# A three-stage decoder layer on one core: the bulk loads of cross-attention move from SyncE's queue to ScalarE's

## The reference

```
x = layernorm(x + attn(x))          # exp sums of causal scores with rotary positions, then a small two-layer net
x = layernorm(x + xattn(x, ctx, ctx, bias, w_out))
x = layernorm(x + ffn(x))           # 512 -> 2048 -> 512, quantised weights and activations, gelu

xattn: q, k, v = heads(x), heads(ctx), heads(ctx)           # no projections of q, k, v
       logits  = q @ k.T + bias                             # bias: 16 x 2048 x 154, the same for all sequences
       attn    = softmax(logits / sqrt(32)) @ v
       return combine(attn) @ w_out
```

## Time and profile before

| | |
|---|---|
| median of three executions | 2286.98 us |
| the profiled execution | 2296.95 us |
| its span, first to last instruction | 2295.1 us |
| TensorE busy | 2126.5 us, 93% |
| VectorE busy | 1738.3 us, 76% |
| ScalarE busy | 1086.7 us, 47% |
| GpSimd busy | 828.9 us, 36% |
| mean granted TensorE clock | 0.947 of full speed |
| DMA queue of SyncE and of stores and loads by GpSimd | 286.07 MB and 160.28 MB |

### The profile page before, as it was taken

One profiled execution on the slowest core, in us unless ns is written; L12 is line 12 of the kernel. 1 busy time (PEld: TensorE's weight loads), 2 busy tenths in 40 slices (PEclk: granted clock), 3 DMA queues, 4 the chain that ended last, 5 costly groups with the idle time before them and its releaser, 6 DMA issues.

```text
span 2295.1 us, 32921 instructions
## 1 busy us (share of the span) xinstructions
PE 2126.5 (93%) x11880; PEld 1184.2 (52%) x11904; DVE 1738.3 (76%) x3296; ACT 1086.7 (47%) x1522; POOL 828.9 (36%) x802
## 2 busy tenths in 40 slices
PE   7999999984898999999999859999999799999997
PEld 3444444431676777776777624444444344444443
DVE  6768686855677798897898665777656488888885
ACT  1444444443355454555555324444444465555551
POOL 2122221222135455555555342322222134444442
PEclk9999999997589899999999779999999899999999
DMA  6344343456669979979996437888888656666662
GB/s 232 107 136 144 103 143 105 114 137 176 179 145 195 251 167 186 264 187 183 254 212 144 152 81 252 289 284 285 272 270 268 250 200 233 226 225 235 228 224 79
DMA packets 386626, 448.46 MB, mean 195 GB/s; under 512 B 279270, under 2 KB 279430, under 8 KB 368032
## 3 DMA queue, kind: packets, MB, share of 16 engines
q1 hardware_dynamic: 322448, 286.07, 46.5%
q0 software_dynamic: 64016, 160.28, 22.9%
HBM read 258.93 MB, written 138.73 MB: 173 GB/s over the span
## 4 chain that ended last, share of the span: by engine, by line
PE 81%; DVE 6%; DMA 5%; issue 5%; ACT 2%; POOL 1%; DVEq 0%; SPq 0%; POOLq 0%; ACTq 0%
PE ps_h L1658 19%; PE ps L1901 19%; PE ps_proj L568 10%; PE ps_o L1230 8%; PE ps_w L1259 6%; PE ps_s L588 5%; DMA qs<-stack 4%; PE ps_o L1226 3%; PE ps_m L1182 3%; PE ps_m L1184 3%; PE ps_l L1208 2%; DVE rope_t L403 1%; PE ps_t L1244 1%; DVE x_hi L386 1%; PE ps_l L1205 1%
## 5 line engine op out<-in xcount | busy, mean ns | idle before, releaser
L1658 PE MATMUL ps_h<-xT,b_rows 128*128 128x512 f16 x2048 | 444.5, 380 | 12.6 <-DMA xT<-x_lo 12.6
L1901 PE MATMUL ps<-w,g_hi 128*128 128x512 f16 x1024 | 389.1, 380 | 21.1 <-DVE g_lo L1837 21.1
L1901 PE MATMUL ps<-w,g_lo 128*128 128x512 f16 x1024 | 389.1, 380 | 0.0
L1658 PEld LDWEIGHTS ps_h<-xT,b_rows 128*128 128x128 f16 x2048 | 200.9, 98 | 256.0 <-issue 16.1
L1230 PEld LDWEIGHTS ps_o<-vm,pT 128*128 128x128 f32 x2048 | 308.9, 208 | 14.1
L1499 ACT ACTIVATE h<-ps_h,b_in_sb,col_scale 128x512 f32<-128x512 f32 x256 | 199.2, 778 | 241.2 <-PE ps_h L1658 241.1
L1060 DVE TENSOR_REDUCE stack<-ps_m 128x2 f16<-128x308 f32 x512 | 244.3, 479 | 73.0 <-PE ps_m L1184 57.9
L1230 PE MATMUL ps_o<-vm,pT 128*128 128x33 f32 x2048 | 292.7, 270 | 0.0
L1017 ACT ACTIVATE pT<-logit 128x512 f32<-128x512 f32 x320 | 199.7, 626 | 126.2 <-DVE logit L1078 124.9
L1572 DVE TENSOR_REDUCE amax_t<-h 128x1 f32<-128x2048 f32 x64 | 146.2, 2284 | 114.2 <-ACT h L1499 113.8
L1750 POOL TENSOR_TENSOR rstd<-vare,minus_half 128x1 f32<-128x1 f32 x64 | 154.4, 2412 | 208.3 <-DVE vare L1855 208.3
(11 more groups left out here) (179 smaller groups left out, 3858.9 us busy)
## 6 DMA issues: line engine op xcount, KB each, us to landing
hidden<-h POOLq DMA_DIRECT2D x64, 1024.0 KB, 6.8
hT<-hidden SPq DMA_DIRECT2D x64, 1024.0 KB, 6.1
xc<-x_cols SPq DMA_DIRECT2D x16, 1024.0 KB, 5.1
xr<-x_rows SPq DMA_DIRECT2D x16, 1024.0 KB, 5.4
x_rows<-x POOLq DMA_DIRECT2D x16, 1024.0 KB, 4.8
x1t<-x_rows SPq DMA_DIRECT2D x64, 256.0 KB, 3.9
bt_main<-bias_main SPq DMA_DIRECT2D x16, 1024.0 KB, 7.1
xres<-x_rows SPq DMA_DIRECT2D x64, 256.0 KB, 3.8
```

What stands on the lines that cost most here:

```text
L1658: mm = pe.matmul(ps_h[f % 4][:], w1[:, c, f * P:(f + 1) * P], xT[:, e, a, :, c, :], start=(a == 0 and c == 0), stop=(a == 1 and c == KC - 1))
L1901: mm = pe.matmul(ps[t][:], g[:, e, f, t * P:(t + 1) * P], w2[:, f, :], start=(f == 0 and a == 0), stop=(f == FC - 1 and a == 1))
```

## The change

ScalarE gets a function `bulk_loads`, called as the last thing of each of its quarters, behind `token_half`. All loads of the bias, of `kb`, `ks` and of the values are issued there, 109 DMAs in all, in the same quarters by number as before, except that the third and fourth group of the first span's bias come in q = -2 and q = -1 instead of (0, 0) and (0, 1). The waits in front of the loads move with them. The very first `kb` and `ks` loads ahead of the pipeline, all transposes, `x1t`, the residual rows and the output weights stay on SyncE.

```diff
             def quarter(s, b, i):                       # SyncE
-                if 4 * n + i == -4:
-                    for j in range(2):
-                        sp.wait_ge(done.x1_out[j], 16 * done.blocks // 2)
-                    sp.wait_ge(done.ks_out, 16 * done.blocks)
-                    sp.wait_ge(done.kb_out, 16 * done.blocks)
-                    load_bias(0, 0)
-                    load_v(0, 0)
-                if 4 * n + i == -3:
-                    load_bias(0, 1)
-                    load_kb(1, 1)
                 turn_heads(*span_at(s, b, i, 6))
                 turn_stack(*span_at(s, b, i, 4))
...
-                if isinstance(s, int) and n == 0 and i < 2:
-                    load_bias(0, 2 + i)
...
-                if i == 0 and not (isinstance(s, int) and n >= UNITS - 2):
-                    sp.wait_ge(mx_done, 32 * (n + 1))
-                    load_kb((b + 2) % BATCH, b % 2)
...
+            def bulk_loads(n, i):                       # ScalarE
+                s, b = n // 4, n % 4
+                if 4 * n + i == -4:
+                    for j in range(2):
+                        act.wait_ge(done.x1_out[j], 16 * done.blocks // 2)
+                    act.wait_ge(done.ks_out, 16 * done.blocks)
+                    act.wait_ge(done.kb_out, 16 * done.blocks)
+                    load_bias(0, 0)
+                    load_v(0, 0)
+                if 4 * n + i == -3:
+                    load_bias(0, 1)
+                    load_kb(1, 1)
+                if 4 * n + i in (-2, -1):
+                    load_bias(0, i)
+                if not 0 <= n < UNITS:
+                    return
+                if i == 0 and n < UNITS - 2:
+                    act.wait_ge(mx_done, 32 * (n + 1))
+                    load_kb((b + 2) % BATCH, b % 2)
+                if i == 1 and not last(n):
+                    if not first(n):
+                        act.wait_ge(pv_done, 8 * n)
+                    load_ks((b + 1) % BATCH, (b + 1) % 2)
+                    load_v((b + 1) % BATCH, (b + 1) % 2)
+                if s < UNITS // BATCH - 1 and b == BATCH - 1 and i >= 1:
+                    act.wait_ge(biased, 5 * (4 * n + i))
+                    load_bias(s + 1, i - 1)
+                if not first(n) and b == 0 and i == 0:
+                    act.wait_ge(biased, 20 * n)
+                    load_bias(s, GROUPS - 1)
...
                 token_half(*at(n, i, 7))
+                bulk_loads(n, i)
```

More of the change, by code:

```diff
@@ L834, in load_residual @@
                     bass.ds(4 * s + t, 1)].rearrange("n p d -> p (n d)")).then_inc(xres_in[t % 2], 16)
[L836 to L840, removed]
             def load_kb(b, e):
@@ L848, in load_ks @@
                 sp.dma_start(ks[3 * HD:STACK, e], rows[3 * HD:STACK]).then_inc(ks_in[e], 16)
-            def load_v(b, e):
-                sp.dma_start(vm[:, e], v_main[b]).then_inc(v_in[e], 16)
-                sp.dma_start(vt[:, e], v_tail[b]).then_inc(v_in[e], 16)
             sp.wait_ge(done.proj_done, done.jobs)
@@ L891, in quarter @@
                     sp.dma_start(x2t[:], w_chunks[:, 2:4]).then_inc(wo_in, 16)
-                if isinstance(s, int) and n >= UNITS:
-                    return
-                if i == 0 and not (isinstance(s, int) and n >= UNITS - 2):
-                    sp.wait_ge(mx_done, 32 * (n + 1))
-                    load_kb((b + 2) % BATCH, b % 2)
[L897 to L901, removed]
-                if not (isinstance(s, int) and s == UNITS // BATCH - 1) and b == BATCH - 1 and i >= 1:
-                    sp.wait_ge(biased, 5 * (4 * n + i))
-                    load_bias(s + 1, i - 1)
-                if not first(n) and b == 0 and i == 0:
-                    sp.wait_ge(biased, 20 * n)
-                    load_bias(s, GROUPS - 1)
             for q in range(-8, TAIL):
@@ L987, in _, with load_bias, load_kb, load_ks @@
         def _(act):
+            def load_bias(s, g):
+                act.dma_start(bt_main[:, g], bias_main[4 * g:4 * g + 4].rearrange("h k (s t) -> k h s t", t=BLK)[
+                    :, :, bass.ds(s, 1), :].rearrange("k h s t -> k h (s t)")).then_inc(bt_in[g], 16)
+                act.dma_start(bt_tail[:, g], bias_tail[g].rearrange("k (s t) -> k s t", t=BLK)[
+                    :, bass.ds(s, 1), :].rearrange("k s t -> k (s t)")).then_inc(bt_in[g], 16)
+            def load_kb(b, e):
+                act.dma_start(kb[:, e], kb_dram[b]).then_inc(kb_in[e], 16)
+            def load_ks(b, e):
+                rows = ks_dram[b].rearrange("r (h k) -> r h k", h=HEADS)
+                act.dma_start(ks[0:3 * HD, e], rows[0:3 * HD]).then_inc(ks_in[e], 16)
+                act.dma_start(ks[3 * HD:STACK, e], rows[3 * HD:STACK]).then_inc(ks_in[e], 16)
+            def load_v(b, e):
+                act.dma_start(vm[:, e], v_main[b]).then_inc(v_in[e], 16)
+                act.dma_start(vt[:, e], v_tail[b]).then_inc(v_in[e], 16)
             def token_half(nu, t):
```

## The result

Four executions of the changed kernel took 2342.70 to 2347.11 us, median **2343.65 us**. Four of the kernel before took 2285.77 to 2302.94 us, median 2292.35 us. The ratio is **1.0227**, 95% interval [1.0193, 1.0261]: slower, as forecast, but 2306 us was forecast and 2340 was the upper end of the range. (The interval lies wholly above 1; whether the loss is more or less than 2% it leaves open.) The profiled execution took 2347.11 us with a span of 2345.3 us, 50.2 us more than before.

What follows compares the result with a forecast made beforehand. TensorE, busy 93% of the span, was taken as the bound. Fill +11 us and steady part +8 us gave 19 us on 2287, so 2306 us; 8-in-10 range 2270 to 2340, the forecast case alone 2295 to 2326.

Steps and rivals of the forecast that it cites:

- The forecast case: Bulk issued after `token_half` falls on the next quarter's transposes, which land late: +19 us, 2306 us, chance 0.5.
- the own queue gives nothing: Bulk on ScalarE's queue does not protect the transposes, which still land about 2.0 us (1.6 to 2.5) after the last bulk load.
- the fill: Pipeline start, q = -4 to -1: no threshold protects, every microsecond of later `stack` landing lengthens the kernel: +11 us.
- the steady part: Quarters after the pipeline start: `stack` landings above 9.0 us after issue stop TensorE: 3.6 us plus about 4 for scatter, +8.
- The rival of fair turns: Transposes in their own queue land in about 8.6 us, stops at the bias change go: 2271 us, chance 0.2.
- ScalarE held at its issues: ScalarE's issues wait while SyncE is occupied by a `stack` transpose, exponentials run late: 2332 us, up to 2380, chance 0.15.
- plus its time to land: In the `stack` landing formula: the last bulk load's time from issue to landing, put at 5.4, 7.0 or 8.0 us.
- The formula: `stack` landing from its issue: last bulk issue's offset behind L997, its landing time, minus 1.4 (transpose's start), plus 2.0 us.
- The twelve (n,1) without bias: Quarters with four bulk issues: next `stack` transpose lands after 8.9 us, just under the 9.0 us threshold; scatter costs perhaps 0.2 us.
- The (3,1) kind: Quarters (3,1), (7,1), (11,1) with six bulk issues: transpose lands after 10.8 us, surplus 1.8 each, net +1.8 us.
- Scatter at the threshold: In 18 steady quarters whose `stack` landings lie near 9.0 us, variation of the landings costs about 4 us.
- The clock: New TensorE stops may lower the granted clock as in 740 to 780 us: up to 10 us more, only in the bounds.

Runs made afterwards that it cites:

- sp_late: Kernel before, with every steady bulk load issued by SyncE one quarter boundary later, just ahead of the next quarter's transposes; fill as before: ratio 1.0161.
- fill_late_sp: Kernel before, with only the pipeline-fill loads issued one quarter boundary later, still by SyncE, right ahead of the transposes: ratio 1.0069.
- kv_act: fill_sp with all bias loads back on SyncE in their old places; ScalarE issues only `kb`, `ks` and the values: ratio 1.0023.
- fill_sp: Changed kernel with the pipeline-fill loads (q = -4 to -1) back on SyncE in their old places; steady bulk stays late on ScalarE: ratio 1.0124.
- act_mid: fill_sp with ScalarE issuing the bulk in the middle of its quarter, between its second and third exponential: ratio 1.0141.
- fill_act: Kernel before, with only the pipeline-fill loads (q = -4 to -1) on ScalarE as in the changed kernel: ratio 1.0083.
- the spread kernel on SyncE: Kernel before, all bulk on SyncE at its old place in the quarter, but loads spread over different quarters: ratios 0.9905 and, run again, 0.9898.

## Why the prediction was wrong in size

**Direction and mechanism held.** The forecast case was that the bulk falls on the next transposes, that the own queue gives nothing, and that the fill loses more than the steady part by quarter. The traces show the late landings, the own queue gained nothing in any run, and the fill holds half of the new idle time (16.1 of 32.6 us). sp_late and fill_late_sp show that a late issue costs as much without the new queue. The rival of fair turns fell: the transposes issued right behind six bulk loads landed in 14.7, 11.8 and 10.3 us, not under 9.0. So did ScalarE held at its issues: they took 0.30 to 0.68 us but for two (0.83 and 1.64 us), `combT` still waits for `ps_t`, and kv_act costs nothing. It happened twice in fill_sp, in (7,2) and (11,2): the sixth issue took 0.75 and 1.05 us, `combT` was 2.3 and 2.6 us late and TensorE idle for 1.2 and 1.6 us.

**The failed term** is "plus its time to land". The formula was offset of the last bulk issue, plus its time to land, minus 1.4, plus 2.0, and I put in the times of before, 5.4, 7.0 and 8.0 us. Those are times of a load that was issued ahead of the transposes of its queue. Handed over with them, the last bias load took 13.9 us instead of 8.0 and `kb` in the fill 10.2 instead of 7.0: the load is drawn out as well as the transpose. (That the DMA engines take turns between them is how I read these landings; no view shows the turns.) The trace of before had a case of it. The forecast used one `b_rows` load, of 8.8 us; all 12 of that line over the whole span show

```profile
DMA to landing us min/median/max: 8.7/13.0/16.5
```

The one of 16.5 us was issued at 697.65, beside the transpose of 697.40 that took 13.41 us. I had read nearly the shortest. The same work took about as long as before: before, the first bulk issue of this place was at 742.66 and the transpose landed at 759.0, 16.3 us; now 766.07 and 783.5, 17.5 us. What was lost is the head start. With the measured times the formula gives the landing, as it must: `token_half` ended at 767.40, the last issue was at +0.7, it landed in 13.9, the transpose stood at +1.4 and landed 1.5 after it: 0.7 + 13.9 - 1.4 + 1.5 = 14.7 us, as the chain shows. The forecast had 2.2 + 8.0 - 1.4 + 2.0 = 10.8: 1.5 too much for the offset, 5.9 too little for the time to land, 0.5 too much behind it. In the fill: `kb` issued at +0.2 behind the end of L976 (570.18), landed in 10.2, transpose at +1.8 and 1.7 after `kb`: 10.3 us, against 8.5 forecast.

Term by term, idle time of TensorE:
- The fill: forecast +11 us. Measured +16.1 us (39.72 against 23.65 us, first rows of the two tables). The four landings grew by 3.7, 6.1, 1.7 and 5.3 us, where 2.8, 4.2, 2.4 and 2.8 stood (the last counted half).
- The steady part: forecast +8 us, measured +16.5. The twelve (n,1) without bias were priced about right or too high: the transposes behind them that no `b_rows` load disturbed landed in 4.3 to 9.8 us, median 7.6, where 8.9 was forecast, and units 5, 9 and 13, which have little else, stood idle 0.6 us at most. The (3,1) kind was too low, 14.7, 11.8 and 10.3 us for 10.8. The loss in the first quarters of units 3, 7 and 11 wasn't in the sum: 9.5, 10.0 and 11.1 us where 8.9, 9.0 and 7.8 were before. Units 3, 7 and 11 hold 11.1 of the 16.5 us by the two tables. In (3,0) `b_rows` now stood 1.7 us ahead of the transpose where it was 0.8 us behind it before; in the other two it isn't so, and no run settles it.
- Scatter at the threshold was 4 us of the sum; nothing in the trace asks for it.

**The clock** was left out of the sum and held for up to 10 us of the bounds. It was 17.3 us in the two profiles, a third of the loss. In the fill the granted clock fell from 0.65 to 0.56, in units 7 and 11 from 0.93 to 0.84 and from 1.00 to 0.93; in unit 3, which has the longest new stop behind the fill, it was 0.87 before and 0.90 after, so not each stop costs clock where it stands. That step, a stop priced as its idle time only, is the second one that failed. The bounds have a slip beside it: their lower end is 2287 + 10 = 2297 us, not 2295.

Sum: 32.6 + 17.3 = 49.9 us measured, 19 forecast. Of the 31 us missing, 5 are the fill, 8 or 9 the steady landings, and 17 the clock.

**What the theory lacked.** That a separate queue gives nothing was too kind. act_mid shows a transpose that was issued ahead of its bulk and took 16.2 us all the same, and at equal amounts of bulk ScalarE is 1.4% behind SyncE. How much of those 1.4% is the queue and how much the later issue isn't separated: the spread was not run on SyncE with late issues.

## What to carry to other kernels

When loads move, ask first at what moment they are handed over and which latency-bound transfer is issued next; price both together as one amount of work from the first issue to the last landing, never with the time that the load took in another place. A queue in order can be a protection: in (3,0), (7,0) and (11,0) SyncE came to its `kb` load only 5.0 to 6.7 us behind the transpose, while a second queue let it start 1.5 us behind. If a bottleneck lies in bursts, spread the bursts (here 1% by moving four loads to other quarters), and price new stops of TensorE with the clock that they cost beside the idle time.

## What the runs showed of the hardware

- **In the trace ScalarE's DMAs leave ahead of its own pending activation.** In the program the issue of line 960 stands behind L976. In the trace it is at 766.07, 0.7 us before L976 starts (766.79) and 1.3 us before it ends. So the bulk came some 1.5 us less late than the forecast assumed.
- **An issue on ScalarE is short**, 0.30 to 0.68 us in 107 of 109. In the changed kernel none of them fell into the time that a `stack` transpose occupies SyncE; in act_mid the `kb` issue of 732.65 did, 3.7 us into 7.30, and took 0.33 us.
- **The clock's low stretch behind the fill varies between executions.** The profiled executions of the kernel before and of the changed one ran unit 1 partly at the lower clock, those of fill_sp, kv_act and fill_act wholly at the upper one. That this isn't the change shows in the spread kernel on SyncE, which was profiled twice. Unit 1 in its first execution and in its second:

```profile
625.82:661.83 36.01, 35.81 (x302) 28.85 (x299) 30.60 (x72) 23.87 (x40) 10.60 (x10) 1.00 0.74 164
...
628.88:674.33 45.45, 45.41 (x317) 36.45 (x316) 32.63 (x74) 23.91 (x40) 10.59 (x10) 0.80 0.60 130
```

The kernel before:

```profile
629.25:674.71 45.46, 45.36 (x317) 36.41 (x316) 32.66 (x74) 24.04 (x40) 10.59 (x10) 0.80 0.62 130
```

  The difference, some 9 us of 2300, is of the size of the spread between executions of one kernel, and 9 of the 10.6 us between the lengths of that kernel in the table (671.9 and 682.5). It is why the ratios above rest on many executions and the lengths of single profiles only illustrate them. It has no part in the 17.3 us: unit 1 took 45.5 us before and 45.4 us after.
